# The ternary FFN's preparation moved into the attention before it, attention tails on separate PSUM banks, and a dispatch whose last batch and names are split

## The chip, the cores and the metric

One core of one Trainium2 chip runs the whole program: TensorE (matmuls and transposes), VectorE, ScalarE, GpSimd (POOL) and the DMA queues, of which SyncE (SP) issues most. The metric is device time in microseconds. The kernel before has a median of 2240.86 us over three runs, from 2239.66 to 2243.93 us.

## The reference

Eight batches of 512 rows of 256 numbers run through four layers, in float32. Each layer has an attention over a short context (64 rows) and a feed-forward part (FFN), each with a layernorm ahead and a residual sum behind:

```
x = x + L0_xcond(norm(x), ctx ...)   # softmax attention, 16 heads
x = x + L0_ffn(norm(x), ...)         # mixture of 8 experts, top 2, own norms, gelu
x = x + L1_xcond(norm(x), ctx ...)
x = x + L1_ffn(norm(x), ...)         # dense, sine terms, relu
x = x + L2_xcond(ctx, norm(x), ...)  # windowed attention
x = x + L2_ffn(norm(x), ...)         # mixture of 8 experts, top 2, gelu
x = x + L3_xcond(norm(x), ctx ...)
x = x + L3_ffn(norm(x), ...)         # ternary, below
```

The last part is the one that the change touches most:

```
def _weight_quant(w):
    scale = 1.0 / clip(mean(abs(w)), 1e-05)
    return clip(round(w * scale), -1.0, 1.0) / scale
def _act_quant(x):
    scale = 127.0 / clip(max(abs(x), axis=-1), 1e-05)
    return clip(round(x * scale), -128.0, 127.0) / scale
gate = silu(act_quant(x) @ weight_quant(w_gate).T)
up   = act_quant(x) @ weight_quant(w_up).T
out  = act_quant(gate * up) @ weight_quant(w_down).T
```

The mean of abs(w) runs over a whole matrix of 256 x 1024 numbers, so the weights can be rounded only when all of them have been summed.

## The kernel before

The rows are cut into 32 tiles of 128 (four to a batch, `TPB`), and x stays in SBUF throughout. The program is a row of stages, "a0 m0 a1 f1 w2 m2 a3 f3": attention, mixture (dispatch and experts), attention, FFN, windowed attention, mixture, attention, ternary FFN. Between two stages all engines meet at a barrier and GpSimd clears semaphores (line 227), so a stage lasts until its last engine is done, and nothing of the next stage starts before. Within a stage every engine has its own list of instructions, in the order in which Python wrote it, and waits on semaphores.

**Attention (line 348).** Step (b, t) takes tile n = 4b + t. TensorE forms the scores of tile n + 1 in two banks `sc_b`, VectorE takes their maxima (758) and subtracts them (761), TensorE turns them (588), ScalarE takes exponents (669), TensorE forms values (548), ScalarE the reciprocals of the sums (652, 654), VectorE multiplies (`scale`, 768), and TensorE projects (`project`, 559) into one bank `out_b`, from which VectorE adds to x (`residual`, 783) and takes the statistics. `project(n)` waits until `residual(n - 1)` has read the bank. After the last step three projections are left (line 617), and each waits for the sum of the one before. In attention 3 the rows of the mixture before arrive beside this: GpSimd and VectorE add them to x (318, 325).

**Attention 0** also feeds the router of the mixture behind it: ScalarE normalises rows (1525), TensorE turns them in the other half of `out_b` (1532), VectorE copies them (772), TensorE forms logits (1543) and VectorE takes them (777). Seven of the eight batches (`AHEAD`) are done so. GpSimd adds a bias to finished rows (`add_post`, 1555) and takes the roots of the last statistics first. The windowed attention w2 has the same router, with ScalarE taking rows and logits.

**Dispatch (line 891)** opens each mixture. It does the last batch (ScalarE normalises 997, TensorE turns 968, ScalarE copies 1001, TensorE forms logits 973) while VectorE selects experts for the first seven, then VectorE ranks everything, and then come eight chunks: VectorE compares tiles (1105) and slots (1107), GpSimd multiplies the first by a number per entry (1021, "names"), ScalarE by the partition's number (1007), TensorE sums (988). The tiles of a chunk alternate between two buffers, and all operands are bf16 in SBUF.

**Experts (1154, 1354)** run 71 tiles, the first gelu of ScalarE preceded by a table load.

**Ternary FFN (line 2235).** Its stage opens with a head: VectorE sums the three weight matrices (2357), normalises the first batch (2298) and finds its scales; TensorE sums over partitions (2493); VectorE clips the three matrices in two passes each (2367, 2368); ScalarE rounds the first batch (2382) and the three matrices (2427). Only then comes the loop: `gate` and `lift` (2448) into one bank pair each, silu (2391), product (2319), maximum (2325), rounding (2395), turning (2464), copy (2400), second layer (2471), residual (2335).

## Time and profile before

| | |
|---|---|
| median of three runs | 2240.86 us |
| the profiled execution | 2244.04 us, its span 2242.2 us |
| TensorE, weight loads | 87%, 65% of the span busy |
| VectorE, ScalarE, GpSimd | 59%, 42%, 27% |
| the two mixtures' experts | 292 to 620 us and 1312 to 1847 us |
| attention 0, 1, 3 | to 243 us, 620 to 868 us, 1847 to 2069 us |
| ternary FFN | 2069 to 2242 us |

The busy shares are averages over eight stages with different limits. Where TensorE is near 100% (the experts) nothing but its own work matters. At every border between stages TensorE stands for 10 to 20 us, and what counts there is a chain through all engines. The chain that ended last is followed back by the profile to 2068.83 us, the barrier before the ternary FFN, and no further; ahead of that the timeline has to be read by stage. PEclk is the granted clock of TensorE: 1.00 is 2.4 GHz, 0.50 is 1.2 GHz.

### The profile page before, as it was taken

The numbers are of one execution on the slowest core, as the hardware profiler recorded it, in microseconds if no ns is written. First come the engines' busy times: TensorE is split into PE (matmuls) and PEld (weight loads), VectorE is DVE, ScalarE is ACT, GpSimd is POOL, SyncE is SP. The second block draws the span as 40 slices with busy tenths as digits, with TensorE's granted clock in tenths as the row PEclk, the third lists the DMA queues.
The fourth block names the chain that finished last, engine by engine and source line by source line (L and its number), as shares of the span: only waits on it lengthen the run. The fifth ranks groups of instructions, "written<-read, shape, count | busy, mean of one in ns | idle before, by whom it ended". The sixth has DMA issues, their size and how long they took to land. (4 is left out here: it accounts for less than half of the span.)

```text
span 2242.2 us, 37690 instructions
## 1 busy us (share of the span) xinstructions
PE 1940.1 (87%) x11915; PEld 1447.4 (65%) x11931; DVE 1318.4 (59%) x3008; ACT 935.3 (42%) x2057; POOL 596.2 (27%) x598
## 2 busy tenths in 40 slices
PE   6999469999848897999979659999999987997687
PEld 3677346666525564566667459999999974664455
DVE  5877656666558886787645542222222216887887
ACT  2544124444346543333224223333333323553787
POOL 1122346666424431011000132222222221321000
PEclk9999579999969998999989669999999997999899
DMA  7000211111141104000001511111111114100001
GB/s 275 11 20 30 78 57 63 61 61 63 51 165 57 57 1 165 0 0 0 0 22 46 197 38 38 36 35 37 37 35 35 37 32 157 39 20 1 10 29 38
DMA packets 71267, 119.68 MB, mean 53 GB/s; under 512 B 13664, under 2 KB 54880, under 8 KB 68096
## 3 DMA queue, kind: packets, MB, share of 16 engines
q1 hardware_dynamic: 55904, 78.89, 10.1%
q0 software_dynamic: 13680, 37.37, 5.2%
q10 hardware_dynamic: 1584, 2.13, 0.3%
q8 instruction: 59, 0.97, 0.2%
q14 instruction: 40, 0.33, 0.0%
HBM read 87.03 MB, written 31.33 MB: 53 GB/s over the span
## 5 line engine op out<-in xcount | busy, mean ns | idle before, releaser
L1440 ACT ACTIVATE e_hT<-psum,x_bt 128x128 f32<-128x128 f32 x568 | 154.6, 384 | 336.4 <-PE psum L1403 331.8
L269 POOL TENSOR_TENSOR rstd<-lnt,half 128x4 f32<-128x4 f32 (+1 forms) x72 | 73.3, 1018 | 778.0 <-DVE lnt L263 778.0
L1403 PEld LDWEIGHTS psum<-e_xT,e_w 128*128 128x128 f32 x2272 | 268.3, 194 | 8.4 <-ACT e_xT L1433 4.9
L1403 PE MATMUL psum<-e_xT,e_w 128*128 128x128 f32 x2272 | 268.9, 277 | 4.2 <-ACT e_xT L1433 4.2
L1412 PE MATMUL psum<-m_w,e_hT 128*128 x1136 | 256.8, 379 | 0.0
L1461 DVE COPY e_w<-m_w 128x2048 f32 x71 | 87.1, 1227 | 238.3 <-PE psum L1403 233.9
L1412 PEld LDWEIGHTS psum<-m_w,e_hT 128*128 128x128 f32 x1136 | 210.4, 190 | 25.7
L758 DVE TENSOR_REDUCE a_mx<-psum 128x8 f32<-128x512 f32 x192 | 123.2, 684 | 80.8 <-PE psum L533 80.3
L1260 ACT ACTIVATE e_hT<-psum,x_bt,x_gt 128x128 f32<-128x128 f32 x284 | 106.9, 457 | 145.0 <-PE psum L1227 145.0
L1344 POOL DMA_INDIRECT rows_out<-e_y,dst x106 | 106.0, 1000 | 208.6 <-DVE e_y L1471 175.0
L1336 POOL DMA_INDIRECT e_x<-rows_in,src x142 | 142.1, 1001 | 56.4 <-issue 35.4
L669 ACT ACTIVATE a_pT<-psum 128x512 f32<-128x512 f32 x192 | 104.1, 593 | 110.5 <-PE psum L588 110.2
L1237 PE MATMUL psum<-m_w,e_hT 128*128 x568 | 143.2, 396 | 4.3 <-ACT e_hT L1260 3.9
L1218 PE MATMUL psum<-m_w,e_xT 128*128 x284 | 137.4, 607 | 1.4 <-ACT e_xT L1252 1.2
L1932 PE MATMUL psum<-f_w,f_q 128*128 128x256 f32 x512 | 121.4, 382 | 14.7 <-DVE f_q L1819 14.7
L1932 PEld LDWEIGHTS psum<-f_w,f_q 128*128 128x128 f32 x512 | 97.0, 191 | 54.7 <-issue 30.5
L761 DVE TENSOR_TENSOR a_pr<-psum,a_mx 128x512 f32<-128x512 f32 x192 | 123.0, 682 | 0.7
L1919 PE MATMUL psum<-f_zT,f_w 128*128 128x512 f32 x256 | 122.6, 605 | 0.8 <-DVE f_q L1816 0.8
L1237 PEld LDWEIGHTS psum<-m_w,e_hT 128*128 128x128 f32 x568 | 103.9, 193 | 22.3 <-issue 5.8
L559 PE MATMUL psum<-att_wo,a_oT 128*128 128x256 f32 x384 | 103.8, 394 | 13.5 <-DVE x_res L783 13.5
L503 PE MATMUL psum<-a_zT,att_wq 128*128 128x512 f32 x192 | 102.3, 659 | 7.2 <-ACT a_qT L646 5.2
L245 DVE BATCH_NORM_STATS2 stats<-x_res 128x6 f32<-128x256 f32 (+1 forms) x256 | 98.8, 419 | 12.3 <-PEq L204 8.7
(298 smaller groups left out, 3559.1 us busy)
## 6 DMA issues: line engine op xcount, KB each, us to landing
m_w<-in_L_ffn_w SPq DMA_DIRECT2D x16, 1024.0 KB, 12.0
m_w<-in_L_ffn_w SPq DMA_DIRECT2D x16, 512.0 KB, 11.9
m_w<-rows_out SPq DMA_DIRECT2D x16, 512.0 KB, 5.9
a_ar_g<-rows_out SPq DMA_DIRECT2D x16, 512.0 KB, 5.1
rows_in<-a_r_z SPq DMA_DIRECT2D x14, 512.0 KB, 2.9
x_res<-in_x SPq DMA_DIRECT2D x8, 512.0 KB, 7.1
m_w<-rows_in SPq DMA_DIRECT2D x8, 512.0 KB, 3.9
out_x<-x_res SPq DMA_DIRECT2D x8, 512.0 KB, 3.0
```

Of the source, the lines that this page charges most:

```text
L758: dve.tensor_reduce(mx[g][:, :], wide[g], AX.X, ALU.max).then_inc(s_max, 1)
L761: dve.tensor_tensor(pr[t % 2][:, g * W:(g + 1) * W].rearrange("p (h l) -> p h l", h=HPC), wide[g], mx[g][:, :, None].to_broadcast([P, HPC, ...
L1218: mm = pe.matmul(h_b[s][:, c * 512:(c + 1) * 512], xT[s][:, kk, :], w1[:, bass.ds(e * (DC * F) + (kk * F + c * 512), 512)], start=(kk == 0 ...
L1237: mm = pe.matmul(y_b[:, 0:D], hT[s][:, f, :], w2[:, bass.ds(e * (FC * D) + f * D, D)], start=(f == 0), stop=(f == FC - 1))
L1260: g = act.activation(hT[s][:, f, :], hT_b[:, f, :], ACT.Gelu, bias=bt[:, col], scale=gt[:, col] if norm else 1.0)
L1336: pool.indirect_dma_start(out=xin[j % 2][:, :], out_offset=None, in_=k.zs[:, :], in_offset=bass.IndirectOffsetOnAxis(ap=k.src[:, j:j + 1], ...
L1344: pool.indirect_dma_start(out=k.ys[:, :], out_offset=bass.IndirectOffsetOnAxis(ap=k.dst[:, j:j + 1], axis=0), in_=y[j % 2][:, :], in_offse ...
L1403: mm = pe.matmul(h_b[s][:, f, :], w1[:, kk, f * P:(f + 1) * P], xT[s][:, kk, :], start=(kk == 0), stop=(kk == DC - 1))
L1412: mm = pe.matmul(y_b[s][:, 0:D], hT[s][:, f, :], k.w2[:, bass.ds(e * (FC * D) + f * D, D)], start=(f == 0), stop=(f == FC - 1))
L1440: g = act.activation(hT[s][:, f, :], h_b[s][:, f, :], ACT.Gelu, bias=bt[:, bass.ds(e * FC + f, 1)])
L1919: mm = pe.matmul(hb[f % HS][:, :], w1[:, kk, f * P:(f + 1) * P], zT[s][:, kk, :], start=(kk == 0), stop=(kk == DC - 1))
L1932: mm = pe.matmul(yb[t % 2][:, 0:D], q[s][:, g, t * P:(t + 1) * P], w2[:, g, :], start=(g == 0), stop=(g == FC - 1))
```

## The change

Seven parts:

1. Ternary head: a class `TernaryHead` holds the buffers of the head, and attention 3 does the head's work. VectorE sums half matrices at t = 1 of batches 1 to 3 and clips at t = 1 of batches 4 to 6; ScalarE rounds half matrices at t = 1 of batches 5 to 7; TensorE adds the totals at tile 16; VectorE normalises the first batch behind tile 27 and takes its scales behind tile 31; ScalarE rounds it after its last reciprocals. The FFN starts with turning, and its table of silu is loaded before the first copy.
2. Tails of all attentions: the last three projections go to `out_b`, `sc_b[0]` and `sc_b[1]`, and don't wait for sums.
3. Tail of attention 0: the last three turned rows go to the banks `tr_b`, ScalarE copies them, logits are taken earlier, and GpSimd adds the bias to finished rows before the last root.
4. Tail of w2: the logits of batch 5 are formed behind tile 0 of the last batch, ScalarE normalises batch 6 between its tanhs, the last two rows use a bank of their own.
5. Dispatch, last batch: each tile has its own bank and semaphore count.
6. Dispatch, names: ScalarE takes the first four of each chunk's eight entries (71 numbers each, scale an immediate) and GpSimd the other four.
7. Both expert stages load the gelu table at their start.

```diff
@@ attention
+        last_b = [out_b, sc_b[0], sc_b[1]]
-                out_norm.root(pool, NB - 1)
                 if router:
                     for r in range(NB - 3, AHEAD):
                         router.add_post(pool, r)
+                out_norm.root(pool, NB - 1)
...
-                def project(n, pairs, t):
+                def project(n, pairs, t, bank=out_b):
                     pe.wait_ge(o_norm, pairs)
-                    wait_pos(pe, x_added, n)
+                    if bank is out_b:
+                        wait_pos(pe, x_added, n)
...
+                        if ternary and n == TPB * 4:
+                            wait_pos(pe, x_added, n - 3)
+                            ternary.totals(pe, out_b)
...
                 for t in range(1, TPB):
-                    project(NT - TPB + t, 2 * NB if t > 1 else 2 * NB - 1, t)
+                    project(NT - TPB + t, 2 * NB if t > 1 else 2 * NB - 1, t, last_b[t - 1])
                     if router and t == 1:
                         router.logits(pe, NB - 3, pr_b[:, D:LG])
                 if router:
-                    pe.wait_ge(x_added, NT)
-                    router.turn(pe, AHEAD * TPB - 1, out_b[:, D:2 * D]).then_inc(y_ps, 1)
-                    router.logits(pe, AHEAD - 1, pr_b[:, D:LG])
+                    first = (AHEAD - 1) * TPB
+                    router.turn(pe, first + 1, rows(0)[:, 0:D])
+                    router.turn(pe, first + 2, rows(0)[:, D:2 * D]).then_inc(late_ps, 1)
+                    router.turn(pe, first + 3, rows(1)[:, 0:D]).then_inc(late_ps, 1)
+                    pe.wait_ge(late_copied, 2)
+                    router.logits(pe, AHEAD - 1, pr_b[:, D:LG], first + 1)
...
+                        if ternary and b > 4 and t == 1:
+                            for i in (0, 1):
+                                ternary.round_weights(act, 2 * (b - 5) + i)
...
+                        if ternary and t == 1:
+                            for i in (0, 1):
+                                if 0 < b < 4:
+                                    ternary.sum_half(dve, 2 * (b - 1) + i)
+                                if 3 < b < 7:
+                                    ternary.clip_weights(dve, 2 * (b - 4) + i)
+                        if ternary and n == NT - TPB - 1:
+                            ternary.normalise(dve, out_norm.done)
+                        if ternary and n == NT - 1:
+                            ternary.scales(dve)
...
-                scale(2 * NB - 1, 1)
                 if router:
                     take_logits(NB - 4)
+                scale(2 * NB - 1, 1)
@@ dispatch
                 for t in range(TPB):
                     n = EARLY + t
-                    o = act.activation(z[:, t * D:(t + 1) * D], k.xt(n), ACT.Identity, bias=k.shift[:, n:n + 1],
-                                       scale=k.rstd[:, n:n + 1])
-                o.then_inc(z_done, 1)
-                act.wait_ge(zT_ps, 1)
-                act.activation(zT[:, :, :], bank[:, :, :], ACT.Copy).then_inc(zT_copied, 1)
+                    act.activation(z[:, t * D:(t + 1) * D], k.xt(n), ACT.Identity, bias=k.shift[:, n:n + 1],
+                                   scale=k.rstd[:, n:n + 1]).then_inc(z_done, 1)
+                    if t > 0:
+                        copy(t - 1)
+                copy(TPB - 1)
...
+                    for i in range(NJ // 2):
+                        act.activation(names[s][:, i, 0, :], at_tile[s][:, i, :], ACT.Copy, scale=1.0 + c * NJ + i)
                     act.activation(names[s][:, :, 1, :], at_tile[s][:, :, :], ACT.Copy,
                                    scale=k.cst[:, C_PART:C_PART + 1]).then_inc(lo_done, 1)
...
-                    pool.tensor_tensor(names[s][:, :, 0, :], at_tile[s][:, :, :], hi, ALU.mult).then_inc(hi_done, 1)
+                    pool.tensor_tensor(names[s][:, NJ // 2:, 0, :], at_tile[s][:, NJ // 2:, :], hi,
+                                       ALU.mult).then_inc(hi_done, 1)
@@ experts, experts_gelu
+                act.preload_act_table_set("gelu_and_others")
@@ window_attention
-                    if b > 0:
+                        if b == NB - 1:
+                            router.normalise(act, (b - 1) * TPB + t, norm.centred)
+                    if 0 < b < NB - 1:
...
+                        if b == NB - 1 and t == 0:
+                            router.logits(pe, NB - 3, tb[:, D:LG])
@@ TernaryHead
+    def sum_half(self, dve, i):
+        j, half = i // 2, i % 2
+        dve.wait_ge(self.k.f3_in, 16 * (j + 1))
+        dve.tensor_reduce(self.wsum[:, half, j:j + 1], self.k.f3_raw[j][:, half * F3:(half + 1) * F3], AX.X, ALU.add,
+                          apply_absolute_value=True).then_inc(self.summed, 1)
...
+    def clip_weights(self, dve, i):
+        j, raw = i // 2, self.k.f3_raw[i // 2]
+        if i % 2 == 0:
+            dve.wait_ge(self.scale_done, 1)
+            dve.tensor_scalar(raw[:, :], raw[:, :], self.wscale[:, j:j + 1], 1.0, ALU.mult, ALU.min).then_inc(self.clip, 1)
+        else:
+            dve.wait_ge(self.clip, j + 1)
+            dve.tensor_scalar(raw[:, :], raw[:, :], -1.0, MAGIC, ALU.max, ALU.add).then_inc(self.clipped, 1)
...
+    def round_weights(self, act, i):
+        j, part = i // 2, slice(i % 2 * F3, (i % 2 + 1) * F3)
+        act.wait_ge(self.magic_set, 2)
+        act.wait_ge(self.clipped, j + 1)
+        act.activation(self.wq["gud"[j]][:, part], self.k.f3_raw[j][:, part], ACT.Identity,
+                       bias=self.down[:, :]).then_inc(self.rounded, 1)
@@ ternary_ffn
-                dve.wait_ge(w_in, 48)
-                for j in range(3):
-                    dve.tensor_reduce(wsum[:, j:j + 1], raw[j][:, :], AX.X, ALU.add,
-                                      apply_absolute_value=True).then_inc(v, 1)
-                n[0] = 3
-                normalise(0, 0, range(TPB))
-                scales(0, 0)
-                dve.wait_ge(tot_ps, 1)
...
-                act.wait_ge(magic_set, 2)
-                round_z(0, 0, range(TPB))
+                act.sem_inc(z_round, TPB)
+                act.preload_act_table_set("silu_and_others")
                 for c in range(DC):
                     copy(0, 0, c)
-                for j, c in enumerate("gud"):
-                    act.wait_ge(w_clip, j + 1)
-                    act.activation(wq[c][:, :], raw[j][:, :], ACT.Identity, bias=down[:, :]).then_inc(w_done, 1)
-                    if j == 1:
-                        act.wait_ge(z_gain, 1)
-                        silu(0, 0, 0)
+                silu(0, 0, 0)
                 silu(1, 1, 0)
                 round_z(1, 1, (0, 1))
```

## Rows read from the trace of the kernel before

**Rows 1.** windows: stretch, us, busy PE, PEld, DVE, ACT, POOL, PEclk
```profile
228.00:243.00 15.00, 9.64 (x33) 7.47 (x33) 3.78 (x16) 0.00 (x0) 5.81 (x4) 0.50 0.07 23
...
1940.00:1980.00 40.00, 36.68 (x312) 25.17 (x311) 34.03 (x94) 21.34 (x43) 12.75 (x14) 1.00 0.17 53
```

**Rows 2.** chain that ended last: start us, us, what
```profile
2068.83 6.67 DVE f_wsum L2357 x3
...
2094.75 1.14 ACT f_h L2395
```

**Rows 3.** timeline, ternary FFN start: start us, us, engine, line, operation, count
```profile
2080.70 1.11 PE L2442 MATMUL psum<-cst,f_z 128*128 128x128 f32 x4 [4.55 <-ACT f_z L2382]
...
2081.84 0.69 ACT L2387 ACTIVATE f_xT<-psum,f_down 128x512 bf16<-128x512 f32 x1 [1.20 <-PE psum L2442]
...
2088.32 1.89 PE L2448 MATMUL psum<-f_wqu,f_xT 128*128 128x512 bf16 x4
...
2089.76 1.11 ACT L2391 ACTIVATE f_g<-psum,f_sg 128x1024 f32<-128x1024 f32 x1
...
2090.91 1.28 DVE L2319 SCALAR_TENSOR_TENSOR f_h<-psum,f_su,f_g 128x1024 f32<-128x1024 f32 x1 [1.22 <-ACT f_g L2391]
...
2090.93 1.04 PE L2448 MATMUL psum<-f_wqg,f_xT 128*128 128x512 bf16 x4 [0.72 <-ACT f_g L2391]
2092.23 1.22 DVE L2325 TENSOR_REDUCE f_hm<-f_h 128x1 f32<-128x1024 f32 x1
```

**Rows 4.** timeline, ends of attention 1 and of attention 3
```profile
863.18 1.10 PE L559 MATMUL psum<-att_wo,a_oT 128*128 128x256 f32 x4 [0.61 <-DVE x_res L783]
...
2060.33 0.69 DVE L768 TENSOR_TENSOR a_oT<-psum,a_rec 128x512 f32<-128x512 f32 x1 [2.23 <-ACT a_rec L654]
...
2063.21 1.75 PE L559 MATMUL psum<-att_wo,a_oT 128*128 128x256 f32 x4 [0.61 <-DVE x_res L783]
```

**Rows 5.** timeline, end of attention 0
```profile
226.04 2.55 PE L1543 MATMUL psum<-gate,a_r_zT 128*128 128x8 f32 x16 [1.01 <-DVE m_lgt L777]
...
231.86 2.05 PE L559 MATMUL psum<-att_wo,a_oT 128*128 128x256 f32 x4 [0.94 <-DVE x_res L783]
...
237.02 3.55 PE L1543 MATMUL psum<-gate,a_r_zT 128*128 128x8 f32 x16 [1.14 <-DVE a_r_zT L772]
...
237.81 4.64 POOL L1555 TENSOR_TENSOR x_res<-x_res,a_r_post_b 128x1024 f32<-128x1024 f32 x2
```

**Rows 6.** timeline, start of the second dispatch
```profile
1262.91 2.07 ACT L997 ACTIVATE r_work<-x_res,shift,rstd 128x256 f32<-128x256 f32 x4 [1.16 <-PEq L227]
...
1267.04 1.02 ACT L1001 ACTIVATE r_work<-psum 128x1024 f32<-128x1024 f32 x1 [2.06 <-PE psum L968]
...
1268.12 3.58 PE L973 MATMUL psum<-gate,r_work 128*128 128x8 f32 x16 [1.11 <-ACT r_work L1001]
```

**Rows 7.** timeline, the chunks of the second dispatch
```profile
1286.02 0.75 DVE L1105 TENSOR_TENSOR r_work<-r_tiles,r_tile 128x568 bf16<-128x568 bf16 x1
...
1286.85 2.05 POOL L1021 TENSOR_TENSOR r_work<-r_work,cst 128x568 bf16<-128x568 bf16 x1 [28.07 <-DVE r_work L1105]
1287.82 1.68 DVE L1105 TENSOR_TENSOR r_work<-r_tiles,r_tile 128x568 bf16<-128x568 bf16 x1
...
1290.56 1.68 DVE L1105 TENSOR_TENSOR r_work<-r_tiles,r_tile 128x568 bf16<-128x568 bf16 x1
```

**Rows 8.** timeline, first tiles of the second mixture
```profile
1324.60 1.28 ACT L1440 ACT_TABLE_LOAD   x1 [5.95 <-PE psum L1403]
...
1328.40 5.46 PE L1403 MATMUL psum<-e_xT,e_w 128*128 128x128 f32 x32 [3.69 <-ACT e_xT L1433]
```

**Rows 9.** timeline: steady batch of attention 3; last logits before dispatch
```profile
1936.03 1.42 POOL L318 TENSOR_TENSOR x_res<-x_res,a_ar_g 128x256 f32<-128x256 f32 x2 [3.55 <-ACT a_ar_g L312]
...
1937.82 1.29 DVE L758 TENSOR_REDUCE a_mx<-psum 128x8 f32<-128x512 f32 x2 [2.26 <-PE psum L533]
...
1257.96 3.55 PE L1543 MATMUL psum<-gate,a_r_zT 128*128 128x8 f32 x16 [0.79 <-issue]
```

171 lines of the change are left out of this document (110 added, 61 removed).

## The prediction

> **What bounds the kernel now.** I read three views in this order. First the windows view, one row for each stretch between two barriers: it shows that the inside of a stage and its border have different limits. In the steady part of attention 3 TensorE works 36.68 of 40 us at full clock, with VectorE at 34.03 and ScalarE at 21.34; in the last 15 us of attention 0 it works 9.64 us at half clock, ScalarE nothing that is recorded, and each engine mostly waits for another [rows 1]. Then the chain that ended last. It begins at 2068.83 us, at the barrier before the ternary FFN, and its first piece is VectorE summing weights for 6.67 us; the first rounding of a hidden tile, where the loop proper begins, comes at 2094.75 [rows 2]. So 25.9 us of this stage are a head. Behind it the chain alternates between ScalarE and TensorE, and the change doesn't touch that. Third, since a chain stops at a barrier, the timeline of every other border that the change touches [rows 4 to 9]. There the question is what ends last, since the next stage waits for all engines.
>
> **Ternary head.** Removed: the whole 25.9 us. What is left before the same mark, from a barrier at 0: turn half a batch 1.11, copy 0.69, turn 1.11, copy 0.69, with some 0.3 of signals, is 3.9 us. Then `gate` at half clock 1.89 (to 5.8) and `lift` 1.89 (to 7.7); silu, 1.11, lies beside the lift. The product takes 1.28 (to 9.0), the maximum 1.22 and its small followers about 0.4 (to 10.7). ScalarE meanwhile waits for the second gate, 1.04 at full clock (to 8.8), does the second silu (to 9.9) and rounds two tiles of the next batch, 1.1 (to 11.0), and only then comes the first rounding [rows 3]. So 11.0 instead of 25.9: 14.9 us gained. The silu table is loaded beside the first turning and costs nothing: the load is 1.28 us where the trace has one [rows 8]. If the clock stays low through the second gate and lift the gain is 13; if it is full from the start, 17.
>
> **What attention 3 pays for it.** Each piece is placed at t = 1, where VectorE, having finished, waits 2.26 us for scores [rows 9]; I counted that hole in each of batches 1 to 5, and it is longer in batch 6. Two half sums are 6.67 / 3 = 2.2 us [rows 2]; two clips I put at 2.5, nearly the same. They fill the hole and run over by 0 to 0.3 us. Queued behind them are the maxima of the next tile, and behind those the TensorE scores of the tile after. ScalarE's two roundings, 2 us, delay its reciprocals, whose reader VectorE comes later anyway. TensorE gets four small matmuls, some 0.5 us, VectorE two small operations ahead of one residual, 0.4. The normalisation behind tile 27 is 1.4 us in a smaller hole. The scales behind tile 31 and ScalarE's rounding of four tiles lie in the 2.23 us in which VectorE waits for the last reciprocals, and beside the tail [rows 4]. Total taken: 1.0 us lost; the bounds are 0 (every hole holds) and 17 (6.7 sums, 7.5 clips, 1.4 and 1.7, all on the path).
>
> A row speaks against the placement: in this very hole GpSimd adds arriving rows, 1.42 us [rows 9], and its operation and VectorE's comparisons stretch each other elsewhere (names, below). The Trainium skill, page "SBUF — State Buffer", section "SBUF: two separate sides", says that the pair of ports shared by VectorE and GpSimd is an exclusive lock held for the whole instruction, taken by VectorE in a two-port mode or with two SBUF inputs. By it each clip of batches 4 and 5 could wait out 1.42 us; no run here shows a clip beside a GpSimd add. Worked from the rows, that is 2 x 1.42 = 2.8 us at most, less what the wait for scores leaves.
>
> **Tails on own banks.** In attention 1 the last projection starts 0.61 us after the one before ended, released by VectorE's sum, and takes 1.10; the last but one waits for a sum too, about 0.4 after its operand is ready [rows 4]. Both waits go: 0.9 us. In attention 3 the same, and the last projection now takes 1.75 because the clock falls in the middle of it [rows 4]; it would end 1 us earlier. I take 1.3 there, 2.2 in all; bounds 1.0 and 3.0. Behind the last sum come statistics, moments and root as before.
>
> **Tail of attention 0.** What ends last is GpSimd: two additions of 4.64 us from 237.81, to 242.45, which stand behind the last root [rows 5]. Moved ahead of it they run from about 225 on, beside TensorE. What is late next is TensorE's line of work. Logits of batch 5 can start about 1 us earlier, since their predecessor was held up only by VectorE's late copy [rows 5]: from 225.1, 2.55, to 227.7. Two projections at half clock, 2.05 each, to 231.8; three turns, 1.9, to 233.7; the second copy, 0.4; logits of batch 6, 3.55, to 237.7; taking them 0.2: 237.9. That gains 4.5 us. With everything at full clock (half of each figure, about) it ends at 234.2 and gains 8. TensorE has fewer waits than before, so I take 5.5.
>
> **Dispatch, last batch (twice).** Before: four normalisations 2.07, turning 2, one copy 1.02, logits 3.58, ending 8.8 us after the stage's start [rows 6]. Now copies of a quarter lie between the normalisations; the last turn ends at about 3.8 us and logits run to 7.4. 1.4 us each, 2.8 in all; bounds 0.5 (the small copies cost ScalarE 0.4 each) and 2.
>
> **Dispatch, names (twice eight chunks).** The first comparison of tiles takes 0.75 us. The next, begun while GpSimd multiplies, takes 1.68 and ends 0.6 after GpSimd; one begins every 2.74 us [rows 7]. So 0.93 us of each chunk is VectorE standing behind GpSimd. GpSimd's 2.05 itself begins beside the slot comparison. Halved, I let it hold VectorE for half of the 0.93: 0.47 a chunk, 3.8 a dispatch, 7.5 in all. If the 2.05 were its own length and no lock were there, all 0.93 would go, 15 in all. The page quoted above is on the side of the lock: the 1.68 agrees with it. ScalarE gets four more short operations beside its old one of 0.77, some 1.6 us, and stays under the period; the lower bound is 3, if each costs 0.4.
>
> **Table loads.** In the second mixture the load of 1.28 us stands between TensorE's first layer and the next tile, and TensorE then waits 3.69 for ScalarE [rows 8]: 1.28 gained. In the first mixture TensorE waits for a row DMA over the same time, so nothing; a bound of 1.3.
>
> **Tail of w2.** The same work in another order: logits of batch 5 move 1.9 us ahead of three output tiles, and the last tanh comes 1.9 later, so the last turn starts at about the old time. 0.2 gained; 1.7 if the last logits, now 3.55 at half clock [rows 9], ran at full clock.
>
> **Sum.** 14.9 - 1.0 + 2.2 + 5.5 + 2.8 + 7.5 + 1.3 + 0.2 = 33.4 us. The profiled execution took 2244.04 us for a span of 2242.2, so it would take 2210.6. It stands 3.2 above the median of the three runs; against the median of 2240.86 the forecast is 2207.5 us.
>
> **Rivals.** *More comes back*: the lock is none and names gain 15, and attention 0 ends at full clock, +2.5 more: 2240.86 - 43.4 = 2197.5. For it: half of a GpSimd operation may leave the comparison untouched altogether. Against: 1.68 fits waiting to the end so well. *Holes don't hold*: in attention 3 TensorE has only 3.3 us in 40 to spare [rows 1], and if half of VectorE's 17 us (and the GpSimd collision) comes on the path, 8 more are lost: 2215.5. *The head is short but the loop starts slow*: the change doesn't do all it says, because silus and rounding of the next batch pile up on ScalarE and the clock is low for the first tiles; 5 lost: 2212.5. *Slower*: the inserted work opens gaps in TensorE's work in attention 3, and its clock falls as it does in rows 1 when it works 9.64 of 15 us. At half clock 40 us of that stage would take about 36.7 more, so from some 37 us at low clock the gain is gone; at twice that, 75 us, 69 are lost and 33.4 gained: 2276. Against it: 36.68 of 40 leaves a long way to 9.64 of 15.
>
> **Chances.** Forecast, within 4 us: 0.50. More comes back: 0.15. Holes don't hold: 0.17. Slow start: 0.12. Slower: 0.02. The rest, 0.04, something I have not seen that leaves about a third of the gain. Eight in ten lie from 2198 to 2217. A measurement can tell about 0.2%, 4.5 us, from no change. Faster 0.96, same 0.02, slower 0.02.
>
> **What would show it.** The first rounding of a hidden tile about 11 us after the last barrier; hardly any VectorE wait for scores at t = 1 of batches 1 to 5, and a batch still every 24 us; GpSimd's last root as its last work in attention 0, logits as the stage's end; comparisons of tiles of about 1.2 us, a chunk every 2.3; no table load inside an expert stage. Wrong would be: a batch of attention 3 longer by over 1 us, a clip far above 1.3 us, a chunk that still takes 2.7 us or is ended by ScalarE.

## The result, and the profile after

The changed kernel takes 2204.65 us (median of four runs, 2204.02 to 2208.59), the kernel before 2241.28 beside it (2239.66 to 2243.93): a ratio of 0.9835, with a 95% interval from 0.9824 to 0.9847, and 36.6 us less. The forecast was 2207.5. The profiled execution took 2205.27 us with a span of 2203.5, against 2242.2 before: 38.7 less. The barriers cut both spans into stages, and their lengths show where it went:

| stage | before | changed | less |
|---|---|---|---|
| attention 0 | 243.35 | 233.11 | 10.24 |
| first mixture: dispatch, experts | 48.54, 328.72 | 42.93, 328.73 | 5.61, 0 |
| attention 1 | 247.49 | 246.74 | 0.75 |
| FFN 1 | 262.14 | 262.14 | 0 |
| w2 | 132.67 | 136.15 | -3.48 |
| second mixture: dispatch, experts | 48.84, 535.79 | 42.91, 532.55 | 5.93, 3.24 |
| attention 3 | 221.25 | 219.36 | 1.89 |
| ternary FFN | 173.41 | 158.88 | 14.53 |

Two lines stand out: attention 0 gained nearly twice the forecast, and w2, which was to gain 0.2, lost 3.5.

The timeline of the changed kernel at the start of the ternary FFN answers [rows 3] (start, length, engine, line, operation, the idle time before it and what ended it):

```profile
2044.62 1.11 PE L2551 MATMUL psum<-cst,f_z 128*128 128x128 f32 x4 [3.96 <-ACTq L2535]
...
2048.62 1.89 PE L2557 MATMUL psum<-f_wqg,f_xT 128*128 128x512 bf16 x4 [0.78 <-ACT f_xT L2501]
...
2052.01 1.91 PE L2557 MATMUL psum<-f_wqg,f_xT 128*128 128x512 bf16 x4
...
2053.71 1.11 PE L2557 MATMUL psum<-f_wqu,f_xT 128*128 128x512 bf16 x4
...
2055.95 1.23 ACT L2509 ACTIVATE f_h<-f_h,f_up,f_hs 128x1024 f32<-128x1024 f32 x1
```

The first hidden tile is rounded at 2055.95, 11.33 us after the barrier at 2044.62, where it was 25.9. The silu table is loaded beside the turning, as was said. The first `gate`, the first `lift` and the second `gate` run at half clock (1.89 to 1.91), and only the second `lift` is near its full speed (1.11).

The end of attention 0, which answers [rows 5]:

```profile
222.29 6.99 POOL L1604 TENSOR_TENSOR x_res<-x_res,a_r_post_b 128x1024 f32<-128x1024 f32 x3
...
224.63 1.85 PE L1592 MATMUL psum<-gate,a_r_zT 128*128 128x8 f32 x16
...
226.33 1.97 PE L569 MATMUL psum<-att_wo,a_oT 128*128 128x256 f32 x8
...
229.70 2.29 PE L1592 MATMUL psum<-gate,a_r_zT 128*128 128x8 f32 x16 [0.74 <-ACT a_r_zT L744]
230.20 1.01 POOL L269 TENSOR_TENSOR rstd<-lnt,half 128x4 f32<-128x4 f32 x1 [0.92 <-DVE lnt L263]
...
232.03 0.19 DVE L805 COPY m_lgt<-psum 128x32 f32<-128x32 f32 x1 [1.91 <-PE psum L1592]
```

The two additions of [rows 5] now follow that of the batch before them (three in the row, to 229.3) and run beside TensorE, and GpSimd's last work is the root, at 231.5. Logits of batch 5 are done by 226.5, both projections take 1.97 together where one took 2.05, and the logits of batch 6 end at 232.0. The difference from [rows 5] is less in the order than in the length of everything of TensorE's: it stays at full clock until 231.2, inside the last logits.

The chunks of the first dispatch, which answer [rows 7]:

```profile
254.09 0.75 DVE L1152 TENSOR_TENSOR r_work<-r_tiles,r_tile 128x568 bf16<-128x568 bf16 x1
254.76 1.22 DVE L1154 TENSOR_TENSOR att_wq<-r_slots,r_slot 128x1024 bf16<-128x1024 bf16 x1
...
254.92 1.58 POOL L1067 TENSOR_TENSOR r_work<-r_work,cst 128x284 bf16<-128x284 bf16 x1 [16.30 <-DVE r_work L1152]
...
255.89 1.21 DVE L1152 TENSOR_TENSOR r_work<-r_tiles,r_tile 128x568 bf16<-128x568 bf16 x1
...
258.16 1.20 DVE L1152 TENSOR_TENSOR r_work<-r_tiles,r_tile 128x568 bf16<-128x568 bf16 x1
```

A comparison of tiles now takes 1.20 to 1.21 us and a chunk 2.26, against 1.68 and 2.73. The first comparison starts 20.98 us after the stage's start in place of 22.79 (20.97 for 23.11 in the second dispatch): the logits of the last batch, which end 8.8 us after the start in [rows 6], end at 7.0.

The tails of attentions 1 and 3 ([rows 4]), from ScalarE's last scaled queries to the barrier, went from 32.31 to 31.08 and from 32.97 to 31.34 us.

In attention 3 the pieces of the head stand in the hole of [rows 9]. A sum in batch 2, and a clip in batch 4:

```profile
1912.87 2.34 DVE L2317 TENSOR_REDUCE f_wsum<-f_rawu 128x1 f32<-128x1024 f32 x2
1913.41 1.42 POOL L318 TENSOR_TENSOR x_res<-x_res,a_ar_g 128x256 f32<-128x256 f32 x2 [3.56 <-ACT a_ar_g L312]
...
1961.14 1.28 DVE L2338 TENSOR_SCALAR f_rawg<-f_rawg,f_wscale 128x2048 f32<-128x2048 f32 x1
1961.43 3.24 POOL L318 TENSOR_TENSOR x_res<-x_res,a_ar_g 128x256 f32<-128x256 f32 x2 [3.56 <-ACT a_ar_g L312]
...
1962.17 1.03 PE L542 MATMUL psum<-a_kb,a_qT 64*128 64x256 f32 x8
1962.45 1.64 DVE L2341 TENSOR_SCALAR f_rawg<-f_rawg 128x2048 f32<-128x2048 f32 x1
1964.01 1.28 DVE L786 TENSOR_REDUCE a_mx<-psum 128x8 f32<-128x512 f32 x2
```

The two half sums take 2.34 us, as the 2.2 of the forecast, and GpSimd's addition beside them its usual 1.42. Beside a clip the addition takes 3.24, and the clip's second pass 1.64. The scores were ready at 1963.2, the maxima begin at 1964.0: the hole is full and 0.8 too small, and yet the next batch starts on time. From the queries of one steady batch to those of the next it is 24.00 to 24.01 us, and 24.12 once, in the stretch from 1960.2 that holds this clip of batch 4.

The bad news is in the tail of w2. ScalarE's last four tanhs in the changed kernel:

```profile
1231.92 0.38 ACT L2191 ACTIVATE a_th<-psum 128x256 f32<-128x256 f32 x1 [1.83 <-PE psum L2275]
1235.83 0.38 ACT L2191 ACTIVATE a_th<-psum 128x256 f32<-128x256 f32 x1 [3.03 <-PE psum L2275]
1238.98 0.38 ACT L2191 ACTIVATE a_th<-psum 128x256 f32<-128x256 f32 x1 [2.28 <-PE psum L2275]
1242.14 0.38 ACT L2191 ACTIVATE a_th<-psum 128x256 f32<-128x256 f32 x1 [2.29 <-PE psum L2275]
```

They are 3.91, 3.15 and 3.16 us apart. In the kernel before they were 1.63, 1.68 and 1.69 apart, the first and the last of them being

```profile
1248.43 0.39 ACT L2142 ACTIVATE a_th<-psum 128x256 f32<-128x256 f32 x1 [1.79 <-PE psum L2221]
...
1253.43 0.39 ACT L2142 ACTIVATE a_th<-psum 128x256 f32<-128x256 f32 x1 [1.30 <-PE psum L2221]
```

So the last four tanhs take 5.2 us more, and what comes behind the last of them takes 7.6 us where it took 9.5, since the logits no longer stand there: together the 3.5 us that the stage lost. The windows of this stretch of the changed kernel (length, then busy time and number of instructions of TensorE, its weight loads, VectorE, ScalarE and GpSimd, the granted clock of TensorE, DMA):

```profile
1230.00:1234.00 4.00, 4.00 (x23) 2.94 (x22) 0.02 (x1) 0.97 (x3) 1.21 (x2) 0.84 0.01 4
1234.00:1238.00 4.00, 4.00 (x11) 2.16 (x10) 0.00 (x0) 0.87 (x2) 0.00 (x0) 0.58 0.00 0
1238.00:1242.00 4.00, 4.00 (x8) 1.90 (x8) 0.00 (x0) 0.87 (x2) 0.00 (x0) 0.50 0.00 0
```

The 0.84 of the first row is the end of a low stretch that the kernel before has too. TensorE is then busy all the time, and yet its clock falls to half within the second row and stays there. What it did before was the moved piece, the sixteen narrow matmuls (8 columns each) of the logits of batch 5, 1.95 us from 1231.76; the clock falls at 1234.7, 2.9 us behind their start. Such a piece does not always do it. The same sixteen matmuls stand in four earlier batches of this stage, from 1171.0, 1184.9, 1198.8 and 1212.7 us, and the granted clock is 1.00 from 1132 to 1228 us. Only behind the fifth, from 1223.9, and 1.5 us in which TensorE waits, comes the low stretch of the first row.

### The profile page after: what moved, and what is told of

Same layout as the page of the kernel before. It is cut to its first block and busy times, and to the rows that moved or that the text cites. A ratio compares the mean times of both kernels' runs of the same rounds, so it can differ in the third digit from the quotient of the medians.

```text
span 2203.5 us, 37784 instructions
## 1 busy us (share of the span) xinstructions
PE 1939.0 (88%) x11932; PEld 1445.1 (66%) x11933; DVE 1310.2 (59%) x3008; ACT 946.0 (43%) x2132; POOL 591.1 (27%) x598
## 3 DMA queue, kind: packets, MB, share of 16 engines
q1 hardware_dynamic: 55904, 78.89, 10.3%
## 5 line engine op out<-in xcount | busy, mean ns | idle before, releaser
L1510 DVE COPY e_w<-m_w 128x2048 f32 x71 | 87.1, 1227 | 231.2 <-PE psum L1451 226.8
L569 PE MATMUL psum<-att_wo,a_oT 128*128 128x256 f32 x384 | 101.4, 388 | 10.4 <-DVE x_res L813 8.4
L598 PE MATMUL psum<-cst,a_pr 128*128 128x128 f32 x768 | 106.2, 283 | 0.2
## 6 DMA issues: line engine op xcount, KB each, us to landing
m_w<-in_L_ffn_w SPq DMA_DIRECT2D x16, 512.0 KB, 12.1
```

The costliest lines, as they stand in the source:

```text
L598: mm = pe.transpose(tr_b[g][:, i, :], pr[t % 2][:, at:at + P], k.ident)
```

## Experiments

Each was timed in rounds with the kernel before; the ratios below are to that. Where an experiment leaves a stage alone, its profile is also one more look at that stage of the changed kernel.

**The whole tail of w2 undone.**

```diff
-                        if b == NB - 1:
-                            router.normalise(act, (b - 1) * TPB + t, norm.centred)
-                    if 0 < b < NB - 1:
+                    if b > 0:
...
-                for half, of in enumerate((rb, bank[:, 0, :])):
-                    take_rows(AHEAD - 1, half, of)
+                for half in range(2):
+                    take_rows(AHEAD - 1, half)
...
-                        if b == NB - 1 and t == 0:
-                            router.logits(pe, NB - 3, tb[:, D:LG])
...
+                router.logits(pe, NB - 3, tb[:, D:LG])
-                for half, to in enumerate((rb, last_rb)):
-                    turn_rows(AHEAD - 1, half, to)
+                for half in range(2):
+                    turn_rows(AHEAD - 1, half)
```

> The changed kernel with the tail of w2 as it was before the change (logits of batch 5 behind the last output tile, one bank for the turned rows, normalisations behind all tanh). In the changed kernel this stage takes 136.15 us instead of 132.67, and the granted clock falls to half in the output tiles that stand behind the moved logits. Theory 1, the moved logits take the clock down: the stage is back at 132.7, the last four output tiles are 1.69 us apart again instead of 3.15, and the time is 2204.65 - 3.5 = 2201.2 us. Rival, the clock falls there for a reason that lies ahead of the tail (the stage starts at another moment): nothing changes, 2204.7 us.

2201.01 us, 0.9835 (0.9808 to 0.9861). The interval is too wide to tell it from the changed kernel, but the stage isn't: 134.28 us, with the tanhs 1.63, 1.68 and 1.69 apart again. That is 1.9 less than 136.15, not 3.5. Most of the rest lies in the tail itself, behind the last tanh: 10.7 us here, 9.5 in the kernel before, which has the same order. The clock falls behind the logits of batch 5 with this order too, 1.6 us behind their start here and 4.7 in the kernel before, so here the turning behind them runs at half clock (1.09 and 1.11 us for 0.63 and 0.66). With the old order the stage took 132.67, 134.28 and 132.81 us in three profiles; with the logits behind tile 0 it took 136.15, 136.15, 136.17, 136.21 and 136.22 in five and 135.42 and 135.93 in two more. Theory 1 holds, in the sense that moving the logits moves the fall ahead of three output tiles; the rival falls.

**Only the logits moved back.**

```diff
-                        if b == NB - 1 and t == 0:
-                            router.logits(pe, NB - 3, tb[:, D:LG])
...
+                router.logits(pe, NB - 3, tb[:, D:LG])
```

> The changed kernel with one piece of the tail of w2 undone: the logits of batch 5 stand behind the last output tile again; the normalisations between the tanh and the second bank for turned rows stay. The last four tanh are 3.9, 3.15 and 3.15 us apart wherever the logits are moved (10.2 us from first to last), and 1.63 to 1.69 (5.0 us) where the whole tail is undone. Theory 1, the moved logits alone take the clock down: 5.0 us from first to last, and the stage takes 132.7 to 134.3 instead of 136.15: 2202 us. Rival, it is the waits that the normalisations put between the tanh: 10 us from first to last, 2204.7 us.

```profile
1229.53 0.38 ACT L2191 ACTIVATE a_th<-psum 128x256 f32<-128x256 f32 x1 [2.08 <-PE psum L2275]
...
1234.53 0.38 ACT L2191 ACTIVATE a_th<-psum 128x256 f32<-128x256 f32 x1 [0.82 <-PE psum L2275]
```

2199.87 us, 0.9811 (0.9796 to 0.9826): its interval just touches that of the changed kernel (0.9824 to 0.9847), so the stage has to decide: 5.0 us from first to last tanh, and 133.29 us for the stage. The normalisations and the second bank cost nothing that shows; moving the logits alone took the time.

**The logits two tiles later.**

```diff
-                        if b == NB - 1 and t == 0:
+                        if b == NB - 1 and t == 2:
```

> The changed kernel with the logits of batch 5 two output tiles later in the tail of w2 (behind t = 2 instead of t = 0; behind t = 3 is the place from before the change). With them behind t = 0 the last tanh are 3.9, 3.15 and 3.15 us apart, with them behind t = 3 they are 1.63 to 1.69 apart. Theory 1, the logits themselves bring the clock down, some 3 us after they begin, wherever they stand: the first two intervals stay at 1.65, the third holds the logits and is 3.7, and everything behind runs at half clock; the stage takes about 134.5 us, 2203 us in all. Rival, it is the time since the idle stretch ahead of the output tiles that counts, not the logits: then the tiles behind t = 0 are slow here too, 3.15 us apart, and the stage takes 136.

```profile
1233.85 0.38 ACT L2191 ACTIVATE a_th<-psum 128x256 f32<-128x256 f32 x1 [1.81 <-PE psum L2275]
...
1237.06 1.95 PE L1592 MATMUL psum<-gate,a_r_zT 128*128 128x8 f32 x16
1237.16 0.38 ACT L2191 ACTIVATE a_th<-psum 128x256 f32<-128x256 f32 x1 [0.82 <-PE psum L2275]
1241.10 0.39 ACT L2191 ACTIVATE a_th<-psum 128x256 f32<-128x256 f32 x1 [3.07 <-PE psum L2275]
```

2202.68 us, 0.9813 (0.9793 to 0.9833). The first two intervals are 1.63 and 1.68, the third, behind the logits, is 3.94. The fall moves with the logits: with them at 1231.76 the clock is at half from 1234.7 on, with them at 1237.06 from 1240.0 on, 2.9 us behind their start both times. The rival, a fixed time since the idle stretch ahead of the output tiles, falls. The stage took 133.12, better than the 134.5 expected.

**GpSimd's order in attention 0 and both table loads undone.**

```diff
+                out_norm.root(pool, NB - 1)
                 if router:
                     for r in range(NB - 3, AHEAD):
                         router.add_post(pool, r)
-                out_norm.root(pool, NB - 1)
...
-                act.preload_act_table_set("gelu_and_others")
...
-                act.preload_act_table_set("gelu_and_others")
```

> The changed kernel with two edits undone that lie in different stages: in attention 0 GpSimd does the last root ahead of its two long additions again, and both mixtures load the gelu table where the first gelu needs it. Attention 0, theory 1: the root ends at 231.4 us, two additions of 2.3 us follow, and the stage ends at 236.1 instead of 232.2: 3.9 us lost. Rival: the additions were never the end, 0. Second mixture, theory 1: what the load costs is not only its 1.28 us but also the clock, which falls because TensorE waits 3.7 instead of 2.4 us ahead of the second tile's first layer (3.8 us long in the changed kernel, 5.5 before): 3.3 us lost. Rival: only the 1.28. First mixture: 0 either way. Together 2204.65 + 3.9 + 3.3 = 2211.9 us; with the second rival 2209.9.

```profile
231.14 4.63 POOL L1602 TENSOR_TENSOR x_res<-x_res,a_r_post_b 128x1024 f32<-128x1024 f32 x2
...
1310.97 5.47 PE L1450 MATMUL psum<-e_xT,e_w 128*128 128x128 f32 x32 [3.69 <-ACT e_xT L1480]
```

2212.94 us, 0.9877 (0.9860 to 0.9893). The tail of attention 0, from ScalarE's last scaled queries to the barrier, takes 40.17 us where the changed kernel has 36.30 (35.97 in its other profiles) and the kernel before 46.30: 4 us hang on the order, as expected. Of the table load its own time is shown, and the part of the clock stays open. TensorE waits 3.69 us for ScalarE ahead of the second tile's first layer, and with the load moved 2.42, 1.27 less. The experts of the second mixture take 535.12 us here, but with the load moved two lengths occur: 532.3 to 532.7 in five profiles, 534.7 to 535.7 in five. The two lengths go with the clock. In the five short ones it rises 10.1 to 10.6 us after the stage's start and stays up; in the five long ones it rises after 12.1 to 13.2 us and falls once more for 3.4 us. So the 3.24 us of the table above holds 1.27 of the load, and the other 2 came and went in kernels that all had the load moved. But a part of the 2 may belong to the load. In this run the clock rises after 10.2 us, as in the short ones, and yet falls once more, and the layer behind the wait takes 5.47 us for 3.84 in the changed kernel. The medians of whole runs (8.3 us lost here, some 4 of them in attention 0) also leave room for more than 1.27. Neither the 1.28 of the rival nor the 3.3 of theory 1 is shown.

**The old banks in the tail of attention 0.** GpSimd keeps the new order; TensorE, ScalarE and VectorE have the old tail (of the edit only TensorE's part is shown).

```diff
-                    project(NT - TPB + t, 2 * NB if t > 1 else 2 * NB - 1, t, last_b[t - 1])
+                    project(NT - TPB + t, 2 * NB if t > 1 else 2 * NB - 1, t, out_b if router else last_b[t - 1])
...
-                    router.turn(pe, first + 1, rows(0)[:, 0:D])
-                    router.turn(pe, first + 2, rows(0)[:, D:2 * D]).then_inc(late_ps, 1)
-                    router.turn(pe, first + 3, rows(1)[:, 0:D]).then_inc(late_ps, 1)
-                    pe.wait_ge(late_copied, 2)
-                    router.logits(pe, AHEAD - 1, pr_b[:, D:LG], first + 1)
+                    pe.wait_ge(x_added, NT)
+                    router.turn(pe, AHEAD * TPB - 1, out_b[:, D:2 * D]).then_inc(y_ps, 1)
+                    router.logits(pe, AHEAD - 1, pr_b[:, D:LG])
...
```

> The changed kernel; in attention 0 alone the tail's projections, turns and router copies are again on one bank as before the change, while GpSimd keeps the new order (additions ahead of the last root). From ScalarE's last scaled queries to the barrier the tail takes 46.3 us before the change, 36.0 to 36.3 in the changed kernel and 40.2 with GpSimd's order undone. Theory 1, most of the gain is TensorE's clock: with the waits for VectorE back the granted clock falls to half as before, TensorE's line ends 1.9 us ahead of where GpSimd ended before, so the tail takes 44.4 and 8.1 us are lost: 2212.8 us. Rival: GpSimd's long additions were what held VectorE and through it TensorE, so the order alone brings nearly all: 37 us, 2205.5 us.

```profile
225.78 1.92 PE L1584 MATMUL psum<-gate,a_r_zT 128*128 128x8 f32 x16 [1.01 <-DVE m_lgt L796]
...
236.02 3.55 PE L1584 MATMUL psum<-gate,a_r_zT 128*128 128x8 f32 x16 [1.15 <-DVE a_r_zT L791]
```

```profile
223.00:226.00 3.00, 1.99 (x21) 1.21 (x10) 1.15 (x4) 2.41 (x5) 3.00 (x2) 1.00 0.01 3
226.00:229.00 3.00, 3.00 (x20) 2.72 (x20) 0.73 (x2) 0.29 (x1) 3.00 (x2) 0.78 0.52 175
229.00:232.00 3.00, 2.06 (x7) 1.31 (x6) 1.18 (x3) 0.00 (x0) 0.26 (x1) 0.50 0.00 0
```

2213.73 us, 0.9870 (0.9855 to 0.9885), the tail 43.90 us: theory 1. TensorE waits 1.01 us for VectorE's copy of the logits (`m_lgt`) and is busy 1.99 of the 3 us in the first window; then the clock falls, to 0.78 in the second and 0.50 in the third. The changed kernel is busy 3.00, 2.96 and 2.29 us in the same windows at 1.00, 1.00 and 0.86. TensorE's last matmul ends at 239.6 instead of 232.0. From the logits of batch 5 to there it is busy 10.85 of 13.79 us, in the changed kernel 6.62 of 7.37: of the 6.4 us between these stretches 4.2 are the same work at a lower clock and 2.2 are waits; the rest of the 7.6 is the later start. The edit brings back waits, copies on VectorE and the fall of the clock together, and no run separates them. The order alone gives 46.3 - 43.9 = 2.4 us, the banks alone 46.3 - 40.2 = 6.1, both 10.0 to 10.3.

**Names: six rows to ScalarE and two to GpSimd, then all eight to ScalarE.**

```diff
-                    for i in range(NJ // 2):
+                    for i in range(6):
...
-                    hi = k.cst[:, C_HI + c * NJ + NJ // 2:C_HI + (c + 1) * NJ, None].to_broadcast([P, NJ // 2, NTILES])
+                    hi = k.cst[:, C_HI + c * NJ + 6:C_HI + (c + 1) * NJ, None].to_broadcast([P, 2, NTILES])
...
```

> The changed kernel, but of the eight rows of names in a chunk GpSimd multiplies two and ScalarE six (four and four before this edit). Theory 1, an exclusive lock: GpSimd waits until VectorE's slot comparison has ended and only then works, 1.0 us for eight rows and 0.52 for four, and VectorE's next comparison waits until it has ended. Then two rows hold VectorE for about 0.27, the comparison of tiles takes 0.98 us instead of 1.20, and a chunk 2.03 instead of 2.26: seven intervals of 0.23 in each of two dispatches, 3.2 us less, 2201.4 us. Rival 1, ScalarE becomes the bound with six short operations and a long one (1.8 us and its signals): the chunk takes 2.2 or more, 2204. Rival 2, the two operations slow each other in proportion without waiting: the comparison is no shorter than 1.1.

> The changed kernel, but ScalarE makes all eight rows of names and GpSimd none. With no GpSimd beside it every comparison of tiles takes 0.75 us (lock or not), and VectorE alone needs 1.80 us a chunk. ScalarE needs 0.26 + 7 x 0.153 + 0.75 = 2.08 us and about 0.1 for signals. Theory 1: ScalarE sets the period, 2.15 to 2.2, so this is hardly better than four and four: 14 x 0.1 = 1.4 us less, 2203.2 us. Rival: the gap between ScalarE and TensorE is hidden by the two buffers, the period is VectorE's 1.80, and 14 x 0.46 = 6.4 us go: 2198.2.

```profile
252.87 1.34 POOL L1067 TENSOR_TENSOR r_work<-r_work,cst 128x142 bf16<-128x142 bf16 x1 [16.31 <-DVE r_work L1152]
253.85 0.97 DVE L1152 TENSOR_TENSOR r_work<-r_tiles,r_tile 128x568 bf16<-128x568 bf16 x1
```

```profile
252.61 0.75 ACT L1052 ACTIVATE r_work<-r_work,cst 128x568 bf16<-128x568 bf16 x1
...
254.48 0.76 ACT L1052 ACTIVATE r_work<-r_work,cst 128x568 bf16<-128x568 bf16 x1
254.59 0.75 DVE L1145 TENSOR_TENSOR r_work<-r_tiles,r_tile 128x568 bf16<-128x568 bf16 x1 [0.30 <-PE psum L1026]
```

(The edit shown is the first one.) Two rows: 2199.73 us, 0.9818 (0.9801 to 0.9834); the comparison takes 0.96 to 0.97 us and a chunk 2.02, on the forecast of 0.98 and 2.03. None: 2198.07 us, 0.9806 (0.9788 to 0.9825); the comparison takes 0.75 and a chunk 2.0 on average, and ScalarE works with hardly a gap, while VectorE waits 0.30 for TensorE, which waits for it. So ScalarE does set most of the period, a little under the 2.15 expected; the last experiment shows the ring that it is part of. The dispatches take 40.8 and 41.0 us in both, against 42.9. Over 8, 4 and 2 rows GpSimd's end lies 1.0, 0.52 and 0.3 us behind the end of the slot comparison, and the next comparison ends 0.6 us behind that.

**The head's pieces one tile later in attention 3.**

```diff
-                        if ternary and t == 1:
+                        if ternary and t == 2:
                             for i in (0, 1):
                                 if 0 < b < 4:
                                     ternary.sum_half(dve, 2 * (b - 1) + i)
...
```

> The changed kernel with VectorE's sums and clips of the ternary weights one tile later in each batch of attention 3 (t = 2, behind the moments, where VectorE goes from one piece of work to the next without a wait). The pieces are 2.34 us (three times) and 2.5 to 2.9 (three times), 15.6 in all. Theory 1, what counts is the place: ahead of t = 2's successor there is no wait to fill, so each piece delays the scores, and only the 1.66 us that TensorE has to spare in a batch of 24.0 takes some back: 15.6 - 6 x 1.66 = 5.6 us lost in attention 3, 2210.3 us; if nothing is taken back 15.6, 2220. Rival, only the sum of the slack in a batch counts and the hole of 2.26 us at the next t = 1 takes the delay: less than 1 us, 2205 us.

```profile
1893.01 1.03 PE L542 MATMUL psum<-a_kb,a_qT 64*128 64x256 f32 x8
1895.25 2.34 DVE L2317 TENSOR_REDUCE f_wsum<-f_rawg 128x1 f32<-128x1024 f32 x2
1897.50 1.28 DVE L786 TENSOR_REDUCE a_mx<-psum 128x8 f32<-128x512 f32 x2
...
1978.10 1.23 DVE L2341 TENSOR_SCALAR f_rawg<-f_rawg 128x2048 f32<-128x2048 f32 x1
```

2222.68 us, 0.9913 (0.9898 to 0.9928): 18 us lost by one tile's distance. Attention 3 takes 237.61 us, 18.25 more. The batches take 26.26, 29.02, 26.26, 27.18 and 27.24 us and the tail 2.4 more than with t = 1, that is 2.3, 5.0, 2.3, 3.1, 3.2 and 2.4 for three pieces of 2.34 and three of 2.5. Scores are ready at 1894.0 and the maxima of that tile begin at 1897.5, behind the sums. Nothing is taken back, neither at the next hole nor by what TensorE has to spare in a batch: the rival and the 5.6 of theory 1 fall, and its 15.6 comes nearest. Three batches lose more than their piece is long, and these are the ones in which TensorE's clock is at half for a stretch: the two with clips lose 0.6 and 0.7 us more, with the clock at half for 3.4 us from 1987.1 and from 2014.4, and the second batch 2.7 more, with the longest such stretch, 6.8 us from 1932.5:

```profile
1928.00:1934.00 6.00, 3.14 (x18) 2.09 (x18) 5.01 (x14) 4.12 (x9) 4.49 (x4) 0.87 0.00 1
1934.00:1940.00 6.00, 6.00 (x26) 4.71 (x23) 4.18 (x8) 3.09 (x7) 1.41 (x2) 0.56 0.00 0
```

Ahead of and into the fall TensorE was busy 3.14 of 6 us. This is how the rival *slower* of the prediction would have begun.

**The changed kernel once more.**

> The changed kernel itself once more. Nine profiled executions so far show stages that no edit of theirs touches with different lengths: attention 0 ahead of its tail 192.6 to 197.1 us, the steady part of attention 1 182.1 to 186.3, the second mixture's experts 532.3 to 535.8. Theory 1, this is where TensorE's stretches at half clock fall in the one execution that is profiled, and it differs from execution to execution of one and the same kernel: this profile shows other lengths than the first of the changed kernel in at least one of the three, by over 1 us, while tails, chunks and the head of the last stage come out within 0.1 us; the median stays within 2 us of 2204.65. Rival, it belongs to the kernel (its instructions' addresses, for one): all three come out within 0.3 us of the first profile.

2206.20 us, 0.9833 (0.9817 to 0.9850). The steady part of attention 1 is 184.92 us where the first profile had 182.76; attention 0 ahead of its tail (196.78 and 196.81) and the second mixture's experts (532.67 and 532.55) agree. Chunks, the tails of attentions 1 and 3 (31.07 and 31.08, 31.34 and 31.34) and the first rounding (11.33) come out the same, the tail of attention 0 0.33 shorter, more than the 0.1 allowed for. So a stage of over 200 us carries an uncertainty of some 2 us in one profile, of one and the same kernel, and a piece of 30 us in which the clock does not fall at a varying place at most a third of a us. (Behind the last tanh of w2, where it does, one and the same order took 9.5 and 10.7 us.)

**A version faster than both.** The whole tail of w2 as before the change, and names seven rows to ScalarE and one to GpSimd.

> The changed kernel with the whole tail of w2 as before the change and the names shared seven rows to ScalarE and one to GpSimd. Two rows on GpSimd gave a chunk of 2.02 us and a comparison of 0.96, none gave 1.99 with ScalarE at work all the time. By the lock one row holds VectorE for about 0.1: a comparison of 0.85, a chunk of 1.91, with ScalarE at 1.84. Theory 1: 14 x 0.35 = 4.9 us less in the two dispatches and 1.9 to 3.5 less in w2: 2204.65 - 7.6 = 2197 us. Rival, ScalarE and its signals set the period as they did with eight rows: 2.0, so 3.6 less and 2198.4 us.

```profile
254.19 1.22 POOL L1067 TENSOR_TENSOR r_work<-r_work,cst 128x71 bf16<-128x71 bf16 x1 [16.28 <-DVE r_work L1152]
255.16 0.85 DVE L1152 TENSOR_TENSOR r_work<-r_tiles,r_tile 128x568 bf16<-128x568 bf16 x1
...
257.22 0.75 DVE L1152 TENSOR_TENSOR r_work<-r_tiles,r_tile 128x568 bf16<-128x568 bf16 x1
```

2197.75 us, 0.9799 (0.9784 to 0.9814): its interval lies below both of the changed kernel's (0.9824 to 0.9847 and 0.9817 to 0.9850), but not below those of the two runs on names and of the logits alone moved back (medians 2199.73, 2198.07 and 2199.87 us), from which it can't be told. The dispatches take 40.24 and 40.49 us (2.7 and 2.4 less) and w2 132.81 (3.3 less). A chunk takes 1.95 us on average over the last six, between the 1.91 of theory 1 and the 2.0 of the rival. The second comparison takes 0.85, as the lock has it; from the third on it begins later and is 0.75 long. What spaces the chunks there is a ring over the two buffers, which the trace shows:

```profile
257.98 1.11 PE L1027 MATMUL psum<-r_work,att_wk 128*128 128x142 bf16 x8 [0.80 <-ACT r_work L1053]
```

TensorE waits 0.80 us for ScalarE's long operation; the comparison that refills the same buffer begins at 259.12, as soon as TensorE has ended (259.09), and ScalarE's next work on it behind that comparison. ScalarE's 1.83, TensorE's 1.11 and the comparison's 0.75 us with some 0.15 for signals are 3.85 us for two chunks, and two chunks take 1.90 + 1.95. With all eight rows on ScalarE the same ring has about 1.98 for ScalarE, 4.0 us in all, and two chunks take 1.87 + 2.11. So the rival was the nearer one in its mechanism: ScalarE sets the period, but in a ring with TensorE and VectorE.

## Why the prediction was right, and where it was off

The measured terms, the small pieces each between marks of their own (so that the clock's wandering in the long stages stays out):

| step | forecast | measured |
|---|---|---|
| ternary head | 14.9 | 14.5 |
| attention 3's loop | -1.0 | -0.1 |
| tails of attentions 1 and 3 | 2.2 | 1.23 + 1.63 = 2.9 |
| tail of attention 0 | 5.5 | 10.0 |
| dispatch, last batch | 2.8 | 1.81 + 2.14 = 4.0 |
| dispatch, names | 7.5 | 3.80 + 3.79 = 7.6 |
| table load | 1.3 | 1.3 |
| tail of w2 | 0.2 | -3.5 |
| sum | 33.4 | 36.7 |

The 36.7 meets the 36.6 between the medians, more closely than the terms are known: the table load's 1.3 is its own length, and what it does to the clock is open. The other 2.0 us between the two spans are the second mixture's.

- *Ternary head*: right. The clock stayed low through the second `gate`, half of the lower bound's case, and so 11.33 stands for 11.0. In the five profiles in which the second mixture's experts took 535 us it rose some 2 us earlier, and the first rounding came at 10.4 to 10.6.
- *Attention 3*: the mechanism was right and even the 1.0 was too much. The hole takes all of it, though a clip overruns it by 0.8. That the place and not the slack counts was only argued; the move to t = 2 shows it, and shows that the upper bound of 17 for pieces off their hole was no exaggeration.
- *The collision there*: beside the clips of batches 4 and 5 GpSimd's addition goes from 1.42 to 3.24 and 2.98 us and the clip's second pass from 1.23 to 1.64 and 1.63. The 1.23 is that of the third clip, which has no addition beside it, and of all three in the run with t = 2. Beside the sums, which read one operand, nothing changes. These rows agree with the rule of the Trainium skill (page "SBUF — State Buffer", section "SBUF: two separate sides"), an exclusive lock for the whole instruction. It cost 0.4 us of VectorE for each of the two clips and not the 1.42 taken as the worst case, since the longer wait fell on GpSimd.
- *Tails*: both waits go in each, and each gained 0.3 more than its term. In attention 3 the clock no longer falls in the last projection (granted clock 0.98 over the stage's last 25 us, 0.89 before; it falls 1.0 us ahead of the stage's end, where it fell 5.3 ahead).
- *Tail of attention 0*: here the size was off by 4.5 us. The step that failed is the choice of value: "TensorE has fewer waits than before" was written down, and yet 5.5 taken, near the half-clock end of 4.5 to 8. With the waits for VectorE's copies back, the clock is back at half (banks undone); that the waits bring it down is likely and not shown apart from the rest of that edit. And the bound was added up wrong: from 225.1, half of each figure but for the copy and the taking ends at 231.8 and not at 234.2, which is a gain of 10.7 us and not 8. The work ended at 232.2.
- *Last batch*: 1.8 to 2.1 for 1.4, at or above the upper bound of 2. The copies of a quarter cost ScalarE 0.38 us and nothing on the path.
- *Names*: right, for a reason that was half a guess. The value was "half of 0.93"; the runs with two rows and none show why it is so: GpSimd waits until the slot comparison ends, works in proportion to its rows (about 0.12 us each), and VectorE waits for it. The rival without any wait, the two slowing each other in proportion, fell with the comparison of 0.96.
- *Table load*: its own time is right (3.69 us of waiting became 2.42). Whether the clock adds to it is open.
- *w2*: the step that failed is "the same work in another order". Where the logits stand sets where TensorE's clock falls, and that sets what runs at half: behind tile 0 the next output tiles as well, at their old place only the turns or the last logits; the rows ahead of the move showed a price only for the other direction (last logits at full clock).

Of the rivals, *more comes back* was right in its half on attention 0 and wrong in its half on the lock; *holes don't hold* and *slow start* did not come. Added up rightly, that half on attention 0 would have been worth 5.2 us and not 2.5. That the total fell 3 us from the forecast is the sum of +4.5, +1.2, +0.9, +0.7, -3.7 and -0.4 and a tenth: better luck than each of the terms. One thing written ahead of the prediction is off: at the borders of the kernel before TensorE stands still for 3.5 to 15.7 us, not for 10 to 20.

## What to carry to other kernels

Price a piece of work put on a busy engine by the place, not by the engine's average: 15 us of VectorE work cost 0.1 us in the hole ahead of a wait and 18 us one tile later. When TensorE has short gaps near the end of a stage, look at the granted clock beside each order of work, and price the tail at both clocks before choosing: the same change doubled one tail's gain by keeping the clock up and lost 3.5 us in another by letting it fall. And compare pieces between marks some 30 us apart rather than whole stages of one profile, and look at where the clock falls in each.

## What the runs showed of the hardware

- In the tail of w2 TensorE's clock fell to half behind the start of sixteen matmuls of 8 columns: 2.7 to 3.1 us behind it in the seven profiles with them behind output tile 0 and 2.9 with them behind tile 2, with TensorE recorded as busy all the time; 1.5 to 4.7 us behind it in the four profiles with them behind the last tile.
- Three such pieces stand in attention 0 between 60 us and its tail. There the clock falls 23 times in the twelve profiles, each time 2.5 to 3.9 us behind the start of such a piece, and never ahead of the first one. One such fall lies in a stretch in which TensorE is busy 23.84 of 24 us (granted clock 0.93 from 174 to 198 us of the changed kernel). Behind 13 of the 36 pieces it does not fall, nor behind the four early ones of w2; and in attention 1, which has no such piece, it falls too. What decides is not settled.
- One and the same code took 182.1 to 186.3 us in twelve profiles (the steady part of attention 1), 192.6 to 197.1 (attention 0 ahead of its tail), and 532.5 or 535 (the second mixture's experts with the load moved); where it was 535, attention 3 and the ternary FFN behind it were 1.5 and 0.8 us shorter.
- GpSimd multiplies of 142 and 71 columns beside VectorE took 1.34 and 1.22 us, of which all but 0.3 and 0.2 lay before the end of the slot comparison.
- ScalarE's operations on 128 x 71 bf16 follow each other every 0.15 us (six in 1.02, eight in 1.33).
